# A graph-attention layer on one core: GpSimd multiplies the rows of the last three jobs by the first scale vector, with its drain behind that and one wait for each scattered tile

## The chip, the cores and the metric

The kernel runs on one core of a Trainium2 chip. The metric is the time of one execution in microseconds on the device. The kernel before was timed in three runs: 673.37, 671.60 and 670.68 us, median 671.6 us.

## The reference

Inputs are 10,000 nodes with rows of 512 floats and 5,000 edges (source, destination) sorted by destination. The layer is attention over the edges, followed by a residual block with layer norms (`n = 10000`, 8 heads of 64):

```python
q, k, v = [(h @ W).reshape(n, H, DK) for W in (Wq, Wk, Wv)]
e = jnp.einsum('ehd,ehd->eh', k[src], q[dst]) / np.sqrt(DK)
attn = softmax of e over the edges of one destination
a = jax.ops.segment_sum(attn[:, :, None] * v[src], dst, num_segments=n).reshape(n, DM)
o = a @ Wo
x = _layernorm(h + o, ln1_g, ln1_b)
f = jax.nn.relu(x @ W1 + b1) @ W2 + b2
y = _layernorm(x + f, ln2_g, ln2_b)
out = _layernorm(h + y)          # without scale and shift
```

(`attn` and the last two lines are written shorter here than in the program.) What matters below is the second half: a norm, a multiplication by `ln1_g`, a small two-layer network, a norm with `ln2_g` and `ln2_b`, the input row added, and a third norm.

## The kernel before

The work is cut into ten rounds of 500 edges. In a round TensorE turns the gathered rows of the destinations and sources, makes q, k, v and the output product O, and the vector and scalar engines do the softmax as scans along the edges. Then the rows go through the residual block in **jobs** of 250 rows, as two tiles of 125 partitions by 512 floats. A round has four jobs: E0 and E1 hold rows of edge destinations, which get the product O added; N0 and N1 hold rows of nodes without an edge. The rows of a job lie in the tile `rows` (`w[n]` in the code) and its input rows in `x_rows` (`xr[n]`), each one buffer for each of the four slots.

The steps of a job, with their lines: the input rows come by an indirect DMA from GpSimd (L575); `norm` or `norm9` makes the first norm (scalar engine L770, or vector engine L1062); `be` adds `ln2_b` to the input rows by an accumulating DMA from GpSimd (L657); `T` turns the normed rows (TensorE L1234) and the scalar engine copies them (L779); `xr` multiplies the rows by `g1_all`, the first scale vector, on the vector engine (L1068, 125x1024 floats at once); `F1` and `F2` are the network (L1263, L1271, and L1251 for the last three jobs) with a relu between them (L788); `x2` adds the network's result from PSUM to the rows (L1074); `sq` takes the squares (L735); `t` takes the mean off and multiplies by `g2_all` (L1083); `y` scales and adds `x_rows` (L1091); `sq3`, then `r3` (L1103), makes the last shift; `z` on the scalar engine (L800) or `z9` on the vector engine (L1097) makes the output rows, tile by tile; `out` scatters them by two indirect DMAs from GpSimd (L579). GpSimd also makes two tensor instructions a round for the softmax mask (L643, L645).

The order of the steps on each engine is written out by hand: the table `PLAN` gives each step ten numbers, one for each round, and an engine runs its steps sorted by them. A name that begins with ">" stands in the last round only, "<" in all but the last, "!" once. Each engine works strictly through its list; semaphores do the waiting between engines. The last three jobs of the program are E0, E1 and N0 of the last round, called **closing** in the code. Their network starts from PSUM banks that a matmul fills with the bias (`B9`, L1247).

`SETTLE` is one step of GpSimd, `pool.drain()` (L626). In the kernel before it stands behind the `be` steps of E0 and E1 of the last round and ahead of the `be` of N0.

The waits that matter below, before (arguments cut; for E1 and N0 of the last round, whose output rows the vector engine makes, the count is `last_rows_done`):

```python
elif what == "x2":
    on.wait_ge("xr_done", nth("dve.xr", slot, i))
elif what == "out":
    on.wait_ge("rows_done", nth("act.z", slot, i))
    for t in range(2):
        scatter(w_wide[n][:, t, :], ...)
```

Of the kernel before, what the change touches and what calls it, by code (L numbers as in the profile page):

```python
# [10 lines left out]
ALU = mybir.AluOpType  # L11
# [78 lines left out]
TXD2 1810 5453 11668 16099 22626 28648 34753 40873 48430 50827;  # L90
TXD3 2014 5783 11716 16147 22674 28987 34801 41303 48478 51070;
# [13 lines left out]
XP 5730 9620 16673 22431 28716 34700 40678 46625 53502 59318;  # L105
# [14 lines left out]
N1.sq 9890 16299 22722 28808 34869 40968 47486 53193 58293 62855;  # L120
<E0.norm 10033 15291 22025 28140 34146 40202 46290 52471 58617;
E1.sq1 10385 16847 22483 28505 34558 40731 47004 52864 59129 63242;
<E0.seed 10527 16746 22960 29055 35090 41733 47244 53401 58881;
N1.ln2 10628 16726 23061 29035 35024 41129 47641 53381 58455 63026;
<E0.T 10648 15710 22272 28358 34434 40562 46888 53006 58982;
E1.ln1 10744 17109 22864 28769 34849 40947 47166 53102 59298 63404;
N1.rs2 10764 17781 23429 29349 35483 41713 48269 53934 58862 63384;
E1.rs1 10836 17155 22915 29156 35070 41110 47199 53362 59513 63449;
<E1.norm 10901 17207 23100 29208 35200 41162 47345 53555 60009;
<E0.F1 11042 17129 22934 29369 35044 40921 47218 53336 59272;  # L130
# [4 lines left out]
N1.rs3 11592 19012 24685 30541 36907 43505 49604 54986 59796 64410;  # L135
# [5 lines left out]
N1.z 12265 19760 25120 31037 38553 43830 49841 55623 59867 64791;  # L141
<N0.seed 12407 18623 24895 30609 37617 43036 48955 55070 59533;
E1.sq 12507 18797 24704 30894 36927 43148 49104 54811 61590 64267;
E0.rs2 12699 18243 24996 30496 36135 42969 48409 55051 59848 64197;
<N0.F1 12770 18772 24611 30516 36427 42944 49315 55025 60463;
E0.sq3 12946 19306 25528 31581 37267 43363 49442 55343 60319 64429;
E0.ln3 13101 20418 25816 31796 37430 43573 49623 55534 60489 64592;
E0.rs3 13169 20451 26086 31829 37930 43762 50173 55603 60581 64933;
E0.z 13221 20576 26423 32292 38733 44282 50226 56199 60696 64985;
E1.ln2 13579 19032 25068 31776 37410 43343 49295 54966 61746 64572;  # L150
E1.rs2 13647 19149 25101 31945 37766 43971 49584 55171 61779 64612;
N0.sq 13857 20257 26105 31964 37998 44092 50516 56057 61159 64649;
E1.sq3 14148 20066 26280 32434 38289 44593 49983 55813 62035 65146;
N0.ln2 14290 20771 26260 32272 38533 44472 50875 56389 61450 64952;
E1.ln3 14310 20718 26565 32616 38444 44807 50934 56510 62190 65301;
N0.rs2 14331 20945 26585 32577 38694 44788 50914 56422 61571 65127;
N0.sq3 14508 21265 26808 32755 38875 45177 51266 56600 61798 65353;
N0.ln3 14671 21420 26964 32910 39037 45527 51550 56976 61953 65509;
E1.rs3 14691 20751 26604 32649 39018 45319 50967 56815 62223 65334;
N0.rs3 14730 21608 27126 32943 39070 45689 51712 57138 62243 65542;  # L160
<E1.z 15149 20803 26984 33010 39151 45547 51408 56996 62288;
# [22 lines left out]
TXD3 2224 5973 11788 16268 23238 29372 35247 41364 48549 51742;  # L184
# [135 lines left out]
def graph_attention(nc, x, src, dst, Wq, Wk, Wv, Wo, g1, be1, g2, be2, W1, b1, W2, b2, out):  # L320
# [7 lines left out]
    R = 125  # L328
# [979 lines left out]
```

## Time and profile before

| | |
|---|---|
| time, median of 3 runs | 671.6 us (670.68 to 673.37) |
| profiled execution, its own time | 670.29 us |
| its span, first to last instruction | 668.6 us |
| TensorE busy | 639.0 us (96%) |
| vector engine busy | 552.5 us (83%) |
| scalar engine busy | 497.8 us (74%) |
| GpSimd busy | 399.5 us (60%) |
| granted TensorE clock, mean | 0.988 of full |

The busy shares are of the span. Times in the text are microseconds from the first instruction of this execution. TensorE is busy nearly all the time until 650 us and not at all after that: the last 19 us are a tail of the three closing jobs and of N1, with the vector and scalar engines at work and GpSimd scattering. A GpSimd row in a timeline is the time in which it makes the descriptors of a DMA, not the transfer.

### The profile page before, as it was taken

To read this page: it belongs to the slowest core of one execution; us is meant where nothing else is said; L and a number is where in the kernel's file an instruction comes from. 1 tells how busy PE (TensorE), PEld (TensorE's weight loads), DVE (VectorE), ACT (ScalarE), POOL (GpSimd) and SP (SyncE) were. 2 spreads that over 40 slices of the span, in tenths; PEclk is the share of its full clock that TensorE was granted. 3 is DMA by queue.
4 is the path that set the end of the run, shared out by engine and by line. 5 is a ranking of instruction groups with operands and counts; after the bars stand their busy time and mean duration, and the time that the engine had idled before them with its cause. 6 is when DMAs were issued, how large, how long until landed. Compare 5 with 4: busy or idle time off the path is not lost.

```text
span 668.6 us, 10865 instructions
## 1 busy us (share of the span) xinstructions
PE 639.0 (96%) x3576; PEld 491.1 (73%) x3576; DVE 552.5 (83%) x1211; ACT 497.8 (74%) x1203; POOL 399.5 (60%) x363
## 2 busy tenths in 40 slices
PE   5999999999999999999999999999999999999980
PEld 3787877777787777777777777777787777777740
DVE  5848879878896898789979887997888799699884
ACT  3334347985868878888879689796987798699884
POOL 8567271665547665767678555566565853856515
PEclk9999999999999999999999999999999999999995
DMA  7864245553644592576464635454774643367553
GB/s 247 215 163 112 58 112 96 150 155 94 170 86 150 161 178 68 187 119 141 127 181 95 139 111 168 117 136 125 167 166 153 178 80 77 109 142 173 151 86 132
DMA packets 38801, 91.48 MB, mean 137 GB/s; under 512 B 9394, under 2 KB 10690, under 8 KB 38746
## 3 DMA queue, kind: packets, MB, share of 16 engines
q0 software_dynamic: 31536, 82.79, 49.5%
q1 hardware_dynamic: 7210, 8.01, 4.6%
q8 instruction: 28, 0.46, 0.3%
q14 instruction: 27, 0.22, 0.1%
HBM read 71.20 MB, written 20.99 MB: 138 GB/s over the span
## 4 chain that ended last, share of the span: by engine, by line
PE 85%; ACT 6%; DVE 3%; POOL 2%; issue 2%; DMA 1%; POOLq 0%; ACTq 0%; DVEq 0%
PE pP L1137 61%; PE pF L1271 5%; PE pT L1197 5%; PE pS L1263 5%; PE pT L1234 5%; ACT squares L735 2%; DMA x_rows<-in_x_dram,node_idx 1%; PE pS L1207 1%; ACT rows L800 1%; PE pS L1283 1%; POOL out_dram L579 1%; ACT nT L779 1%; PE pP L1283 1%; ACT rows L770 1%; POOL xd L575 1%
## 5 line engine op out<-in xcount | busy, mean ns | idle before, releaser
L735 ACT ACTIVATE squares<-rows,sums 125x512 bf16<-125x512 f32 x200 | 142.4, 715 | 28.9 <-DVE rows L1091 14.0
L575 POOL DMA_INDIRECT x_rows<-in_x_dram,node_idx x40 | 47.4, 1186 | 71.6 <-DVE rows L1091 51.3
L575 POOL DMA_INDIRECT x_rows<-in_x_dram,edge_idx x40 | 46.9, 1171 | 51.6 <-DVE rows L1091 28.3
L657 POOL DMA_DIRECT2D x_rows<-in_L_gnn_ln_b_dram x40 | 52.8, 1459 | 31.7 <-DVE rows L1003 12.2
L1137 PE MATMUL pP<-wo_hi,aT_hi 128*125 128x512 f32 x160 | 65.9, 412 | 0.0
L1137 PE MATMUL pP<-xTd_hi,wq_hi 128*128 128x500 f32 x160 | 64.3, 402 | 0.8 <-DVE xTd_lo L941 0.8
L1137 PE MATMUL pP<-xTs_hi,wv_hi 128*128 128x500 f32 x160 | 64.8, 405 | 0.0
L1137 PE MATMUL pP<-xTs_hi,wk_hi 128*128 128x500 f32 x160 | 63.1, 394 | 0.0
L1137 PE MATMUL pP<-wo_lo,aT_hi 128*125 128x512 f32 x160 | 63.1, 394 | 0.0
L1137 PE MATMUL pP<-xTs_hi,wk_lo 128*128 128x500 f32 x160 | 63.0, 393 | 0.0
L1137 PE MATMUL pP<-wo_hi,aT_lo 128*125 128x512 f32 x160 | 62.9, 393 | 0.0
L1137 PE MATMUL pP<-xTs_hi,wv_lo 128*128 128x500 f32 x160 | 62.6, 391 | 0.0
L1137 PE MATMUL pP<-xTd_hi,wq_lo 128*128 128x500 f32 x160 | 62.6, 391 | 0.0
L579 POOL DMA_INDIRECT out_dram<-rows,node_idx x40 | 45.8, 1145 | 27.8 <-ACT rows L800 16.6
L1137 PE MATMUL pP<-xTd_lo,wq_hi 128*128 128x500 f32 x160 | 62.3, 389 | 0.0
L1137 PE MATMUL pP<-xTs_lo,wk_hi 128*128 128x500 f32 x160 | 62.1, 388 | 0.0
L1137 PE MATMUL pP<-xTs_lo,wv_hi 128*128 128x500 f32 x160 | 62.1, 388 | 0.0
L1091 DVE SCALAR_TENSOR_TENSOR rows<-rows,rs,x_rows 125x512 f32<-125x512 f32 x80 | 57.2, 753 | 4.5 <-DMA x_rows<-in_L_gnn_ln_b_dram 1.8
L800 ACT ACTIVATE rows<-rows,shift,rs 125x512 f32<-125x512 f32 x76 | 57.4, 806 | 4.5 <-DVE shift L1103 4.4
L575 POOL DMA_INDIRECT xd<-in_x_dram,dst_idx x36 | 48.9, 1359 | 19.7 <-issue 10.2
L579 POOL DMA_INDIRECT out_dram<-rows,edge_idx x40 | 43.6, 1090 | 26.9 <-ACT rows L800 16.7
L1083 DVE SCALAR_TENSOR_TENSOR rows<-rows,nmean,g_all 125x512 f32<-125x512 f32 x80 | 56.6, 749 | 2.8 <-ACT squares L735 2.7
(190 smaller groups left out, 1721.0 us busy)
## 6 DMA issues: line engine op xcount, KB each, us to landing
x_rows<-in_L_gnn_ln_b_dram POOLq DMA_DIRECT2D x40, 512.0 KB, 7.2
dst_row<-in_dst_dram SPq DMA_DIRECT2D x9, 250.5 KB, 3.5
q<-in_L_gnn_Wq_dram SPq DMA_DIRECT2D x1, 1024.0 KB, 5.7
rows<-in_L_gnn_Wk_dram SPq DMA_DIRECT2D x1, 1024.0 KB, 9.0
rows<-in_L_gnn_Wv_dram SPq DMA_DIRECT2D x1, 1024.0 KB, 6.1
x_rows<-in_L_gnn_Wo_dram SPq DMA_DIRECT2D x8, 128.0 KB, 8.1
x_rows<-in_x_dram,node_idx POOLq DMA_INDIRECT x40, 3.6
edge_idx<-fill_nodes,fill_idx POOLq DMA_INDIRECT x40, 3.2
```

Of the source, the lines that this page charges most:

```text
L575: pool.indirect_dma_start(rows, None, x, bass.IndirectOffsetOnAxis(ap=table[:, column:column + 1].bitcast(U32), axis=0), bounds_check=N - ...
L579: pool.indirect_dma_start(out, bass.IndirectOffsetOnAxis(ap=table[:, column:column + 1].bitcast(U32), axis=0), rows, None, bounds_check=N ...
L657: pool.dma_start(xr_wide[n], bass.AP(tensor=be2.tensor, offset=be2.offset, ap=[[0, P], [0, 2], [1, D]]), accum_op=ALU.add).then_inc(s[f"be ...
L735: ins = act.activation(squares[:, t, :], w[n][:, t, :], ACT.Square, scale=-float(D), bias=sums[c][n][:, t:t + 1], accum_out=sq[c][n][:, t: ...
L800: ins = act.activation(w[n][:, t, :], w[n][:, t, :], ACT.Identity, scale=rs[3][n][:, t:t + 1], bias=shift[n][:, t:t + 1])
L1083: ins = dve.scalar_tensor_tensor(w[n][:, t, :], w[n][:, t, :], nmean[n][:, t:t + 1], g2_all[0:R, :], ALU.add, ALU.mult)
L1091: ins = dve.scalar_tensor_tensor(w[n][:, t, :], w[n][:, t, :], rs[2][n][:, t:t + 1], xr[n][:, t, :], ALU.mult, ALU.add, accum_out=sums[3][ ...
L1137: ins = pe.matmul(acc, left(a, k), right(b, k), start=(k == 0 and a == b), stop=(k == KC - 1 and a == 1))
L1197: ins = pe.transpose(pT_of(i, step)[:, R * t:R * t + R], rows[0:R, t, P * k:P * k + P], ident[0:R, 0:R])
L1234: ins = pe.transpose(pT_of(i, step, half)[:, 2 * R * c + R * t:2 * R * c + R * t + R], w[n][:, t, P * (2 * half + c):P * (2 * half + c) + ...
L1263: ins = pe.matmul(hidden(i, slot)[DFF * t:DFF * t + DFF, :], w1[:, k, :], nT[:, k, R * t:R * t + R], start=(k == 0), stop=(k == KC - 1))
L1271: pe.matmul(f_banks(i, slot)[t][0:R, :], hT_of(i, slot)[DFF * t:DFF * t + DFF, :], w2[DFF * t:DFF * t + DFF, :], start=False, stop=True, s ...
```

## The change

Three things are changed, and the numbers of some steps in `PLAN`, which leave the order on TensorE and the scalar engine as it was.

1. `xr` of E0, E1 and N0 in the last round goes from the vector engine to GpSimd, as a step `xr9` with the same operands (125x1024, both inputs in SBUF), counted on a new semaphore that `x2` of these jobs waits for.
2. On GpSimd the steps now stand E0.xr9, E1.xr9, N0.be, N0.xr9, SETTLE, where SETTLE, N0.be stood.
3. `z` and `z9` count each of their two tiles, and each scatter waits for its own tile. This holds for all ten rounds.

```diff
-E0.xr 10768 15670 22546 28841 34825 40884 47195 53117 59047 63190;
+<E0.xr 10768 15670 22546 28841 34825 40884 47195 53117 59047;
...
-E1.xr 11526 17991 23735 29917 36131 42296 48107 54331 60995 63745;
+<E1.xr 11526 17991 23714 29917 36131 42296 48107 54331 60995;
...
->SETTLE 63423
+>E0.xr9 63423;
+>E1.xr9 63722;
+>N0.xr9 64005;
+>SETTLE 64107
...
+    late_rows = [(i, step.split(".")[0]) for i, step in sequence("pool") if step.endswith(".xr9")]
...
     elif what == "z":
         for t in range(2):
-            ins = act.activation(w[n][:, t, :], ...)
-        ins.then_inc(s["rows_done"], 1)
+            act.activation(w[n][:, t, :], ...).then_inc(s["rows_done"], 1)
...
+    elif what == "xr9":
+        on.wait_ge("all_loaded", 32)
+        on.wait_ge("turned", 2 * nth("pe.T", slot, i))
+        pool.tensor_tensor(w[n], w[n], g1_all[0:R, :].rearrange("p (a d) -> p a d", a=1).broadcast_to([R, 2, D]), ALU.mult)\
+            .then_inc(s["last_xr_done"], 1)
     elif what == "out":
-        if ("dve.z", slot, i) in steps_done:
-            on.wait_ge("last_rows_done", nth("dve.z", slot, i))
-        else:
-            on.wait_ge("rows_done", nth("act.z", slot, i))
         for t in range(2):
+            if ("dve.z", slot, i) in steps_done:
+                on.wait_ge("last_rows_done", 2 * nth("dve.z", slot, i) + t - 1)
+            else:
+                on.wait_ge("rows_done", 2 * nth("act.z", slot, i) + t - 1)
             scatter(...)
...
     elif what == "x2":
-        on.wait_ge("xr_done", nth("dve.xr", slot, i))
+        if (i, slot) in late_rows:
+            on.wait_ge("last_xr_done", late_rows.index((i, slot)) + 1)
+        else:
+            on.wait_ge("xr_done", nth("dve.xr", slot, i))
```

How it moves the instructions on GpSimd, at the end of the program. The slots are N0, N1, E0, E1; a scatter of `rows,node_idx` is N1's or N0's, of `rows,edge_idx` E0's or E1's. The drain is no row in these lists. Before, it stands between the second and the third DMA of L657:

```order
L657 DMA x_rows<-in_L0_gnn_ln2_b_dram 128x2x512 [waits hx_done] x2
L657 DMA x_rows<-in_L0_gnn_ln2_b_dram 128x2x512 [waits n1_done]
L579 DMA out_0_dram<-rows,node_idx 10000x512 [waits rows_done]
L579 DMA out_0_dram<-rows,node_idx 10000x512
L579 DMA out_0_dram<-rows,edge_idx 10000x512 [waits rows_done]
L579 DMA out_0_dram<-rows,edge_idx 10000x512
L579 DMA out_0_dram<-rows,edge_idx 10000x512 [waits last_rows_done]
```

And with the change, where the drain stands behind the last multiplication (line numbers are four higher):

```order
L661 DMA x_rows<-in_L0_gnn_ln2_b_dram 128x2x512 [waits hx_done] x2
L666 TENSOR_TENSOR rows<-rows,g1_all 125x1024 [waits turned,all_loaded]
L666 TENSOR_TENSOR rows<-rows,g1_all 125x1024 [waits turned]
L661 DMA x_rows<-in_L0_gnn_ln2_b_dram 128x2x512 [waits n1_done]
L666 TENSOR_TENSOR rows<-rows,g1_all 125x1024 [waits turned]
L583 DMA out_0_dram<-rows,node_idx 10000x512 [waits rows_done] x2
L583 DMA out_0_dram<-rows,edge_idx 10000x512 [waits rows_done] x2
L583 DMA out_0_dram<-rows,edge_idx 10000x512 [waits last_rows_done] x2
```

The three multiplications stand where GpSimd had only the drain, N0's `be` comes after two of them, and every scatter row has its own wait.

On the vector engine, from `x2` of E0 (buffer 2) over `y` of N1 (1) and `t` of E0 to `x2` of E1 (3). Before:

```order
L1074 SCALAR_TENSOR_TENSOR rows,sums2_2<-pF1,rows 125x512 [waits f_filled,xr_done]
L1074 SCALAR_TENSOR_TENSOR rows,sums2_2<-pF0,rows 125x512 [waits f_filled]
L1068 TENSOR_TENSOR rows<-rows,g1_all 125x1024 [waits turned]
L1078 TENSOR_SCALAR nmean2<-sums2_2 125x2 [waits x2_done]
L1091 SCALAR_TENSOR_TENSOR rows,sums3_1<-rows,rs2_1,x_rows 125x512 [waits be_added_N1,rs2,t_done]
L1091 SCALAR_TENSOR_TENSOR rows,sums3_1<-rows,rs2_1,x_rows 125x512
L1083 SCALAR_TENSOR_TENSOR rows<-rows,nmean2,g2_all 125x512 [waits sq2,nm2]
L1083 SCALAR_TENSOR_TENSOR rows<-rows,nmean2,g2_all 125x512
L1074 SCALAR_TENSOR_TENSOR rows,sums2_3<-pP0,rows 125x512 [waits f_filled,xr_done]
L1074 SCALAR_TENSOR_TENSOR rows,sums2_3<-pP1,rows 125x512 [waits f_filled]
```

With the change:

```order
L1086 SCALAR_TENSOR_TENSOR rows,sums2_2<-pF1,rows 125x512 [waits f_filled,last_xr_done]
L1086 SCALAR_TENSOR_TENSOR rows,sums2_2<-pF0,rows 125x512 [waits f_filled]
L1090 TENSOR_SCALAR nmean2<-sums2_2 125x2 [waits x2_done]
L1103 SCALAR_TENSOR_TENSOR rows,sums3_1<-rows,rs2_1,x_rows 125x512 [waits be_added_N1,rs2,t_done]
L1103 SCALAR_TENSOR_TENSOR rows,sums3_1<-rows,rs2_1,x_rows 125x512
L1095 SCALAR_TENSOR_TENSOR rows<-rows,nmean2,g2_all 125x512 [waits sq2,nm2]
L1095 SCALAR_TENSOR_TENSOR rows<-rows,nmean2,g2_all 125x512
L1086 SCALAR_TENSOR_TENSOR rows,sums2_3<-pP0,rows 125x512 [waits f_filled,last_xr_done]
L1086 SCALAR_TENSOR_TENSOR rows,sums2_3<-pP1,rows 125x512 [waits f_filled]
```

One row, the multiplication of E1 (L1068), is gone, and `x2` waits for GpSimd's count in its place. The multiplication of E0 is gone in the same way ahead of this piece and that of N0 behind it; nothing else moves.

## Rows read from the trace of the kernel before

**Rows 1.** By stretch, the last: busy us of PE, PEld, DVE, ACT, POOL; clock, DMA share, GB/s

```profile
650.00:669.00 19.00, 0.00 (x0) 0.00 (x0) 9.40 (x25) 9.64 (x28) 8.44 (x8) 0.56 0.43 134
```

**Rows 2.** Section 4 of the page, the chain that ended last, by engine

```profile
PE 85%; ACT 6%; DVE 3%; POOL 2%; issue 2%; DMA 1%; POOLq 0%; ACTq 0%; DVEq 0%
```

**Rows 3.** Timeline of GpSimd (POOL), 632 to 669 us: start, length, instruction, idle before

```profile
633.88 2.76 POOL L657 DMA_DIRECT2D x_rows<-in_L_gnn_ln_b_dram  x2
647.84 1.20 POOL L657 DMA_DIRECT2D x_rows<-in_L_gnn_ln_b_dram  x1 [11.20 <-issue]
655.01 1.11 POOL L579 DMA_INDIRECT out_dram<-rows,node_idx  x1 [5.96 <-ACT rows L800]
656.41 1.43 POOL L579 DMA_INDIRECT out_dram<-rows,node_idx  x1 [0.30 <-issue]
...
663.31 0.98 POOL L579 DMA_INDIRECT out_dram<-rows,node_idx  x1 [0.30 <-issue]
664.60 0.98 POOL L579 DMA_INDIRECT out_dram<-rows,node_idx  x1 [0.30 <-issue]
```

**Rows 4.** Timeline of the vector engine (DVE), 632 to 669 us

```profile
638.68 1.00 DVE L1062 TENSOR_SCALAR rows<-rows,rs,nb 125x512 f32<-125x512 f32 x2
...
640.96 0.69 DVE L1074 SCALAR_TENSOR_TENSOR rows<-pF,rows 125x512 f32<-125x512 f32 x1 [1.27 <-PE pF L1251]
...
643.39 0.75 DVE L1091 SCALAR_TENSOR_TENSOR rows<-rows,rs,x_rows 125x512 f32<-125x512 f32 x1
...
644.73 1.41 DVE L1083 SCALAR_TENSOR_TENSOR rows<-rows,nmean,g_all 125x512 f32<-125x512 f32 x2
...
646.06 0.69 DVE L1074 SCALAR_TENSOR_TENSOR rows<-pP,rows 125x512 f32<-125x512 f32 x1
...
648.62 1.23 DVE L1068 TENSOR_TENSOR rows<-rows,g_all 125x1024 f32<-125x1024 f32 x1
...
649.88 0.69 DVE L1074 SCALAR_TENSOR_TENSOR rows<-pF,rows 125x512 f32<-125x512 f32 x1
...
660.27 1.00 DVE L1097 TENSOR_SCALAR rows<-rows,rs,shift 125x512 f32<-125x512 f32 x2
```

**Rows 5.** Timeline of the scalar engine (ACT), 632 to 669 us

```profile
647.40 0.72 ACT L735 ACTIVATE squares<-rows,sums 125x512 bf16<-125x512 f32 x1
...
651.23 0.72 ACT L735 ACTIVATE squares<-rows,sums 125x512 bf16<-125x512 f32 x1 [0.23 <-DVE rows L1074]
...
652.65 1.50 ACT L800 ACTIVATE rows<-rows,shift,rs 125x512 f32<-125x512 f32 x2
```

**Rows 6.** Timeline of TensorE (PE), 632 to 669 us

```profile
640.78 1.07 PE L1234 MATMUL pT<-ident,rows 125*128 125x125 f32 x8
...
648.57 1.13 PE L1251 MATMUL pF<-w,hT 64*125 64x512 f32 x4
```

**Rows 7.** The two drains on GpSimd's sequencer: ns min/median/max, start

```profile
L626 POOLq DRAIN  x1: 11954/11954/11954, 635.4 to 635.4; - x1
...
L336 POOLq DRAIN  x1: 799/799/799, 667.5 to 667.5; - x1
```

**Rows 8.** Tile x_rows, 630 to 669 us, landings; then the traffic of one microsecond

```profile
DMA to landing us min/median/max: 6.4/7.4/8.3
...
643.00:644.00 1.00, 1.00 (x18) 0.83 (x13) 1.00 (x3) 1.00 (x5) 0.00 (x0) 1.00 0.02 4
```

**Rows 9.** Timelines of POOL and DVE at 436 and at 202 us

```profile
436.17 0.63 POOL L643 TENSOR_SCALAR far<-nsame 128x500 f32<-128x500 f32 x1
436.25 1.09 DVE L1091 SCALAR_TENSOR_TENSOR rows<-rows,rs,x_rows 125x512 f32<-125x512 f32 x1
...
202.76 0.61 POOL L645 TENSOR_SCALAR nsame<-nsame 128x500 f32<-128x500 f32 x1
202.78 0.69 DVE L1074 SCALAR_TENSOR_TENSOR rows<-pF,rows 125x512 f32<-125x512 f32 x1 [1.59 <-PE pF L1271]
```

**Rows 10.** One line of GpSimd, a memset of one column

```profile
L595 POOL MEMSET eps_col<- x1: 99/99/99, 11.2 to 11.2; 128x1 f32 x1
```

More of the change, by code:

```diff
@@ new lines @@
+E0.ln3 13101 20418 25816 31796 37430 43573 49623 55534 60489 64586;
+E0.rs3 13169 20451 26086 31829 37930 43762 50173 55603 60581 64910;
+E0.z 13221 20576 26423 32292 38733 44282 50226 56199 60696 64962;
+E1.ln2 13579 19032 25068 31776 37410 43343 49295 54966 61746 64566;
+E1.rs2 13647 19149 25101 31945 37766 43971 49584 55171 61779 64606;
+N0.sq 13857 20257 26105 31964 37998 44092 50516 56057 61159 64626;
+E1.sq3 14148 20066 26280 32434 38289 44593 49983 55813 62035 65123;
+N0.ln2 14290 20771 26260 32272 38533 44472 50875 56389 61450 64929;
@@ L222 @@
 G2 6883 11707 19807 25839 32991 37180 44037 50514 57738 62263;
-N0.sum 6978 15086 22739 28241 33332 40308 46610 52459 57533 62648;
+N0.sum 6978 15086 22719 28241 33332 40308 46556 52431 57533 62648;
 N1.sum 7097 11847 19279 25139 31297 38205 43462 50087 54799 59980;
@@ new lines @@
+N1.r3 11713 19740 24783 30973 38331 43581 49636 55073 59828 64556;
+<N0.xr 12083 18222 23848 31417 36018 42541 49369 54445 60428;
+E1.x2 12303 18469 24418 30458 36533 42962 48679 54676 61225 64106;
+E0.t 12426 17794 24109 30782 35886 42830 48984 54919 59842 63925;
+E1.m2 12558 19025 24600 30653 36668 43454 49482 55332 61540 64364;
+E0.y 12791 18832 25382 30987 37046 43144 49235 55198 60118 64230;
+E0.r3 13201 20557 26232 31861 38355 44177 50206 55800 60613 64942;
+E1.t 13268 19458 25516 31869 37245 43664 49644 55351 61746 64564;
@@ L264 @@
+N0.x2 13552 19956 25648 31663 37830 43914 50273 55871 60797 64433;
+N0.m2 13734 20624 25851 31798 38363 44185 50578 56287 60979 64696;
+E1.y 13742 19606 26097 32138 38012 44043 49835 55542 61889 64707;
+N0.t 14012 20975 26260 32273 38430 44408 50795 56307 61407 64950;
+N0.y 14363 21119 26663 32609 38727 44960 51120 56454 61606 65136;
+E1.r3 14723 20783 26922 32983 39132 45280 51045 56847 62255 65343;
+N0.r3 15549 21708 27158 32975 39124 45796 51861 57671 62486 65551;
 >E0.norm9 62887;
 >E1.norm9 63501;
->E1.z9 65386;
@@ L267 @@
->N0.z9 65593
+>E1.z9 65363;
+>N0.z9 65570
 """,
@@ L799, in _ @@
                         for t in range(2):
[L800 to L802 removed]
+                            act.activation(w[n][:, t, :], w[n][:, t, :], ACT.Identity,
+                                                 scale=rs[3][n][:, t:t + 1], bias=shift[n][:, t:t + 1])\
+                                .then_inc(s["rows_done"], 1)
         @block.vector
```

175 lines of the change are left out of this document (75 added, 100 removed).

## The prediction

> **What bounds the kernel now.** Read the stretches first: until 650 us TensorE sets the pace, and in the last 19 us it has nothing to do, while the vector engine (DVE) is busy for 9.4 us, the scalar engine (ACT) for 9.6 and GpSimd for 8.4 [rows 1]. The chain of waits over the whole span is TensorE's to 85% [rows 2]. The change touches rounds 1 to 9 only by the finer wait of the scatters, and no row of TensorE waits for a scatter there, so I cost that part at nothing: what covers it is TensorE's own work. All that can move the time lies behind 635 us.
>
> There, read GpSimd from the end backwards. The eight last scatters start at 655.01, and each begins 0.30 us after the one before has ended, a pitch of 1.29 us; the last ends at 665.6 [rows 3]. They are a queue with no hole. The output rows of N0, which feed the seventh, are complete at 661.3 [rows 4], but that scatter starts at 663.31 [rows 3]: the data is 2 us early, the queue is the bound. So the end is the **start of the first scatter plus 10.6 us**. The first one waits for N1's `z`, two tiles on ACT from 652.65 to 654.15 [rows 5]. It starts 0.86 us later, the cost of the wait and of the issue.
>
> What sets 652.65 is ACT's list: squares of E1's `x2` from 647.40, of E0's `y`, then squares of N0's `x2` at 651.23, then `z` [rows 5]. Those wait for DVE, which does E0's `t` at 644.73, E1's `x2` at 646.06, E0's `y`, the multiplication of N0 at 648.62 and N0's `x2` at 649.88 [rows 4]. TensorE gives N0's product between 648.57 and 649.7 [rows 6], so `x2` of N0 can't come earlier whatever DVE is spared.
>
> **The scatter waits for its own tile.** `z` of N1 makes its first tile in half of 1.50 us. The first scatter can start 0.7 us earlier, if GpSimd is free and nothing else moves. The second tile is ready well before the second scatter. **Gain 0.7 us.**
>
> **The multiplications leave DVE.** Three times 1.15 us (1.23 busy at 648.62, less what overlaps with the next instruction [rows 4]). Before 640.96 DVE waited for TensorE 1.27 us anyway; of the second, 644.73 would become 643.97 at best, but E1's `x2` needs a product of TensorE that comes just before 646; the third is spared where TensorE holds `x2` back until 649.7 [rows 6]. **Gain at most 0.1 us**, and I count nothing.
>
> **The multiplications on GpSimd: length.** The trace has no tensor instruction with two inputs on GpSimd. The nearest is the mask, one input of 500 columns in 0.61 us [rows 9], with a fixed part of about 0.1 [rows 10]; so 0.5 us for 500 columns and 1.0 for 1024. With one read that is 1.1 us (lower end: 1.2 by plain proportion); if two inputs are read one behind the other 2.15; upper end 2.5, twice the plain proportion. I take **2.2 us**, because each column needs two reads. The Trainium skill (GPSIMD Engine Reference, Performance versus the Vector engine) gives 4497 ns for a two-input add of 2048 fp32 columns; half of it is 2.25 us, and the sum would then be 0.1 us larger.
>
> **What they block.** At 436.25 a DVE instruction with two inputs in SBUF took 1.09 us beside a mask of GpSimd that ended at 436.80, where the row at 643.39 takes 0.75: it began after the mask, and the next mask waited for it. At 202.78 `x2`, which reads PSUM and one SBUF operand, took its usual 0.69 beside the other [rows 4, 9]. So in this kernel `t`, `y`, `r1` and `r3` exclude a GpSimd tensor instruction, `x2` does not. The Trainium skill says this too (SBUF — State Buffer, SBUF: two separate sides): the port pair is an exclusive lock, "the other fully blocks". By a sharing of bandwidth the delays below would be small; by this rule they are whole instructions, and the trace agrees (1.09 against 0.75).
>
> Now walk through the tail, with 2.2 us for each:
> - E0: GpSimd is free at 636.64 [rows 3], multiplies until 638.85. E1's norm on DVE (638.68 to 639.68 [rows 4]) ends 0.4 later, at 640.1; TensorE turns those rows at 640.78 [rows 6]. Cost 0.
> - E1: its rows are turned at 641.85 [rows 6]; GpSimd works from 641.9 to 644.1. DVE's `y` of N1 starts at 644.2 in place of 643.39 [rows 4].
> - N0: `be` is issued first (1.25 us), to 645.4; then GpSimd waits for the second tile of `y` and works from 645.55 to 647.75. E0's `t` moves from 644.73 to 647.75: **3.0 us later**. E1's `x2` starts at 649.1 (+3.0), E0's `y` follows; N0's `x2` starts at 651.75, not 649.88 (+1.9, since the 1.15 us of its own multiplication is gone).
> - ACT: squares of E1 at 650.35 in place of 647.40, of E0's `y` at 651.9, then two logarithms and an exponential, and squares of N0 at 653.9, not 651.23. `z` of N1 starts at 655.3: **2.65 us later**. All behind it moves as much; N0's output tile is there at 663.5, the seventh scatter comes at 665.2.
>
> So the first scatter starts at 655.3 + 0.75 + 0.86 = 656.9, not 655.01: 2.65 - 0.7 = **1.9 us later**, and the queue of eight behind it is as long as before.
>
> **The drain.** Before, it stands for 11.95 us from 635.4, and GpSimd is held until 647.84 [rows 3, 7]. Nobody missed it. It now begins at 647.75, when N0's work is done, with the first scatter behind it. Two readings fit. (a) It waits for transfers: the last `be` was issued at 635.4 and landed within 8.3, at 643.7, where traffic ends [rows 8]; then 3.6 us pass to 647.34. With that, N0's `be`, issued near 644.1, lands at the latest at 651.5 (the median, 7.4 [rows 8]) and the drain ends by 655.1, the scatters could start at 655.6. It hides behind `z`. Cost 0. (b) Its 10.7 us after 636.64 are its own work. Then it ends at 658.45. The other drain, with ten DMAs since and all landed, took 0.8 us [rows 7], which fits either. I take (a), since the drain outlasts the transfers by so little; it isn't well founded.
>
> **Sum.** -0.7 - 0 + 2.65 + 0 = **+1.9 us**: the profiled execution of 670.3 us would be 672.2. It is 1.3 below the median of the runs, 671.6, so the forecast is **673.5 us**. A measurement here can tell about 0.5% (3.4 us) from no change; the forecast is slower, but within it.
>
> **Rivals.**
> 1. *The drain is work of its own (b), slower.* The first scatter starts at 658.45 + 0.5 = 658.95 (the 0.5 lies between the old drain's end and the next DMA), 2.0 after my forecast, but the queue then runs with less DVE work beside it: 7 pitches of 1.29 and 0.98 give 669.0 against 665.6, so +3.4 us, 675.0. With 2.5 us for a multiplication it is +4.0. For it: eleven us for some 350 DMAs and 0.8 for ten. Against it: why end just behind the landings? It decides as soon as the drain ends after 656.4. Chance 0.30.
> 2. *GpSimd and DVE don't hold each other up in this form, faster.* Then only the early tile is left: -0.7 us, 670.9. The 1.09 us row speaks against it. Chance 0.07.
> 3. *The multiplication is as fast as one read, 1.2 us.* E1's `x2` is then about 1 us late, N0's not at all; ACT's chain slips 0.6, the tile gives 0.7 back: 671.6, no change. Chance 0.08.
> 4. *It takes over 3 us*, E1's norm reaches TensorE late and both later ones grow: +4 to +5 us, 676. Chance 0.05.
> My forecast has the remaining 0.50.
>
> **The numbers.** The cases within 0.5% are the forecast (673.5, 2.5 us a piece gives 674.1), rivals 2 and 3, and nearly half of rival 1, which lies on the edge: 0.50 + 0.07 + 0.08 + 0.13, less 0.08 for a longer multiplication or a disturbed median, and less 0.03 for a gain I see no way to. That gives same 0.67, slower 0.30, faster 0.03. The range goes from rival 2, 670.8, to rival 1 at 2.5 us and some spread, 676.2.
>
> **What would show it.** In the profile after: three tensor instructions on GpSimd of about 2.2 us near 636.7, 641.9 and 645.6; E0's `t` starting when the third ends; a first scatter near 657 behind N1's first tile by 0.86. If the drain ends after that tile, rival 1 holds. If `t` of E0 starts at 644 and takes its usual 1.4 us, the exclusion is wrong. If the scatters have holes between them, the output rows and no longer the queue are the bound, and my sum is too small.

## The result and the profile after

The changed kernel takes 674.23 us (median of 22 runs), the kernel before 672.09 us in the runs beside it. The ratio is **1.0035, with a 95% interval of 1.002 to 1.0051**: by the ratio 2.4 us slower (the medians differ by 2.1), inside the 0.5% that the prediction called "same". The forecast was 673.5 us.

The profiled execution after has a span of 675.2 us, 6.6 more than the one of before. Not all of that is the change. This execution reached the turning of E0's rows in the last round at 638.24 us; other kernels below, which up to there are the same but for single steps off the chain, at 633.6 to 637.6. The start of the program shows most of the rest: long before the three jobs that are changed, TensorE was granted 0.94 of the full clock on average in one execution and all of it in the other, and in the same 60 us it got through 276 matmul instructions against 301. The first 60 us of the kernel after with the part of them at half the clock (1.2 and not 2.4 GHz), then the first 60 us of the kernel before, from the view by stretches (columns: start:end, length, busy us of PE, PEld, DVE, ACT, POOL with counts, granted TensorE clock, DMA share, GB/s):

```profile
0.00:60.00 60.00, 47.48 (x276) 38.21 (x277) 35.20 (x89) 18.53 (x33) 40.75 (x49) 0.94 0.75 191
...
42.79:49.62 6.83, 6.05 (x15) 4.87 (x16) 0.65 (x1) 0.72 (x2) 5.38 (x6) 0.50 0.64 166
```

```profile
0.00:60.00 60.00, 51.29 (x301) 41.32 (x302) 39.10 (x96) 21.52 (x39) 41.48 (x49) 1.00 0.69 191
```

The other executions fit this. Three, the one of before among them, have no such stretch of half clock near 43 us and reach the turning at 633.6 to 634.1; ten have one of 3.4 us and reach it at 635.5 to 637.6; this one has 6.8 us and reaches it at 638.24.

So I read everything from one mark: the start of TensorE's turning of E0's rows in the last round, 634.14 us before and 638.24 after:

```profile
634.14 1.02 PE L1234 MATMUL pT<-ident,rows 125*128 125x125 f32 x8
```

```profile
638.24 1.02 PE L1246 MATMUL pT<-ident,rows 125*128 125x125 f32 x8
```

Times "from the mark" below are differences to it, and **the stretch** is the time from it to the end of the last scatter: 31.44 us before, **34.07 after, +2.63**. It repeats to 0.01 us between executions of kernels that do the same there (34.07, 34.07, 34.07, 34.06 and 34.07 in five), where whole executions differ by 5 us. Behind the last scatter 2.9 to 3.0 us remain in both.

GpSimd after, from its timeline (columns as in [rows 3]):

```profile
639.50 1.24 POOL L661 DMA_DIRECT2D x_rows<-in_L_gnn_ln_b_dram  x1 [0.79 <-PE pT L1246]
640.29 2.84 POOL L666 TENSOR_TENSOR rows<-rows,g_all 125x1024 f32<-125x1024 f32 x1
646.08 2.38 POOL L666 TENSOR_TENSOR rows<-rows,g_all 125x1024 f32<-125x1024 f32 x1 [2.95 <-PE pT L1246]
648.39 1.19 POOL L661 DMA_DIRECT2D x_rows<-in_L_gnn_ln_b_dram  x1
649.17 2.80 POOL L666 TENSOR_TENSOR rows<-rows,g_all 125x1024 f32<-125x1024 f32 x1
661.67 1.12 POOL L583 DMA_INDIRECT out_dram<-rows,node_idx  x1 [9.70 <-ACT rows L809]
663.09 1.04 POOL L583 DMA_INDIRECT out_dram<-rows,node_idx  x1 [0.30 <-issue]
...
671.33 0.98 POOL L583 DMA_INDIRECT out_dram<-rows,node_idx  x1 [0.30 <-issue]
```

The row that has the engine to itself takes 2.38 us. The two of 2.84 and 2.80 us begin while the row of `be` ahead of them still runs; from its end they take 2.39 too. The eight scatters are a queue without a hole again.

The vector engine after (as [rows 4]; L1095 is `t`, L1090 `m2`, L1103 `y`, L1086 `x2`, L1071 the norm):

```profile
639.38 4.31 DVE L1095 SCALAR_TENSOR_TENSOR rows<-rows,nmean,g_all 125x512 f32<-125x512 f32 x2
...
643.86 1.00 DVE L1071 TENSOR_SCALAR rows<-rows,rs,nb 125x512 f32<-125x512 f32 x2
645.05 0.69 DVE L1086 SCALAR_TENSOR_TENSOR rows<-pF,rows 125x512 f32<-125x512 f32 x1 [0.19 <-PE pF L1263]
...
646.40 2.08 DVE L1090 TENSOR_SCALAR nmean<-sums 125x2 f32<-125x2 f32 x1
648.39 0.74 DVE L1103 SCALAR_TENSOR_TENSOR rows<-rows,rs,x_rows 125x512 f32<-125x512 f32 x1
...
649.06 3.47 DVE L1103 SCALAR_TENSOR_TENSOR rows<-rows,rs,x_rows 125x512 f32<-125x512 f32 x1
...
652.46 1.40 DVE L1095 SCALAR_TENSOR_TENSOR rows<-rows,nmean,g_all 125x512 f32<-125x512 f32 x2
653.79 0.68 DVE L1086 SCALAR_TENSOR_TENSOR rows<-pP,rows 125x512 f32<-125x512 f32 x1
...
656.36 0.16 DVE L1090 TENSOR_SCALAR nmean<-sums 125x2 f32<-125x2 f32 x1
656.43 0.68 DVE L1086 SCALAR_TENSOR_TENSOR rows<-pF,rows 125x512 f32<-125x512 f32 x1
```

Each multiplication on GpSimd has a long row beside it: `t` of N1 takes 4.31 us for two tiles (usual 1.41, [rows 4]), `m2` of E0, an instruction of two columns, 2.08 (0.16 at 656.36), and the **second tile of N1's `y` 3.47 (usual 0.75)**. Behind that come `t` of E0, `x2` of E1 at 15.55 us from the mark (11.91 before) and `x2` of N0 at 18.19 (15.74 before).

The scalar engine after (as [rows 5]; L744 are squares, L809 is `z`):

```profile
652.57 0.72 ACT L744 ACTIVATE squares<-rows,sums 125x512 bf16<-125x512 f32 x1 [3.09 <-DVE rows L1103]
...
655.12 0.72 ACT L744 ACTIVATE squares<-rows,sums 125x512 bf16<-125x512 f32 x1 [0.50 <-DVE rows L1086]
...
660.03 1.50 ACT L809 ACTIVATE rows<-rows,shift,rs 125x512 f32<-125x512 f32 x2
```

It waits 3.09 us for that second tile, then 0.50 for `x2` of E1, and from there it is busy without a gap until `z` of N1, which starts 21.79 us from the mark (18.51 before, +3.28). The first scatter starts 1.64 us after `z`, not 2.36, since it waits for one tile only. 3.28 less 0.72 is **+2.6 us**, the whole difference. No `x2` waited for GpSimd's product: E1's, at 653.79, is ready at 648.46, and N0's, at 656.43, at 651.97.

The two drains of GpSimd's sequencer after (as [rows 7]):

```profile
L630 POOLq DRAIN  x1: 9670/9670/9670, 648.8 to 648.8; - x1
```

```profile
L339 POOLq DRAIN  x1: 709/709/709, 674.3 to 674.3; - x1
```

The first ends at 658.52, 2.3 us before the first output tile is there. It costs nothing. Whether it waits for landings or has work of its own this row doesn't say: the landing of N0's `be`, 654.51, is 4.0 us before its end, and GpSimd was free 6.55 us before it.

### The profile page after: what moved, and what is told of

The parts are those of the page before. It is cut to its first block and busy times, and to the rows that moved or that the text cites. A ratio compares the mean times of both kernels' runs of the same rounds, so it can differ in the third digit from the quotient of the medians.

```text
span 675.2 us, 10866 instructions
## 1 busy us (share of the span) xinstructions
PE 639.8 (95%) x3576; PEld 491.9 (73%) x3576; DVE 555.9 (82%) x1208; ACT 497.6 (74%) x1203; POOL 409.6 (61%) x366
## 5 line engine op out<-in xcount | busy, mean ns | idle before, releaser
L744 ACT ACTIVATE squares<-rows,sums 125x512 bf16<-125x512 f32 x200 | 142.3, 715 | 31.2 <-DVE rows L1103 16.5
L1103 DVE SCALAR_TENSOR_TENSOR rows<-rows,rs,x_rows 125x512 f32<-125x512 f32 x80 | 59.7, 783 | 3.8 <-issue 1.4
L1095 DVE SCALAR_TENSOR_TENSOR rows<-rows,nmean,g_all 125x512 f32<-125x512 f32 x80 | 59.0, 778 | 2.8 <-ACT squares L744 2.6
L809 ACT ACTIVATE rows<-rows,shift,rs 125x512 f32<-125x512 f32 x76 | 57.4, 806 | 4.6 <-DVE shift L1115 4.4
L1086 DVE SCALAR_TENSOR_TENSOR rows<-pF,rows 125x512 f32<-125x512 f32 x78 | 50.4, 683 | 8.4 <-PE pF L1283 8.2
```

Of the source, the lines that this page charges most:

```text
L744: ins = act.activation(squares[:, t, :], w[n][:, t, :], ACT.Square, scale=-float(D), bias=sums[c][n][:, t:t + 1], accum_out=sq[c][n][:, t: ...
L809: act.activation(w[n][:, t, :], w[n][:, t, :], ACT.Identity, scale=rs[3][n][:, t:t + 1], bias=shift[n][:, t:t + 1])\
L1086: dve.scalar_tensor_tensor(w[n][:, t, :], f_banks(i, slot)[t][0:R, :], 1.0, w[n][:, t, :], ALU.mult, ALU.add, accum_out=sums[2][n][:, t:t ...
L1095: ins = dve.scalar_tensor_tensor(w[n][:, t, :], w[n][:, t, :], nmean[n][:, t:t + 1], g2_all[0:R, :], ALU.add, ALU.mult)
L1103: ins = dve.scalar_tensor_tensor(w[n][:, t, :], w[n][:, t, :], rs[2][n][:, t:t + 1], xr[n][:, t, :], ALU.mult, ALU.add, accum_out=sums[3][ ...
```

## The experiments

The theory was: a tensor instruction of GpSimd holds the vector engine up (exclusion), for its whole length, and the queue of eight scatters carries the delay of `z` to the end; the drain waits for landings and is hidden. The rivals: the delay comes from `x2` waiting for GpSimd's product; the drain is work of its own; nothing is excluded. The tile waits and the last kernel below were timed in twelve runs a series; the others ran once, and only their traces are read.

### The tile waits alone

The kernel before with the third part of the change: `z` and `z9` count each tile and each scatter waits for its own.

```diff
-ins.then_inc(s["rows_done"], 1)
+act.activation(w[n][:, t, :], ...).then_inc(s["rows_done"], 1)
...
+on.wait_ge("rows_done", 2 * nth("act.z", slot, i) + t - 1)
```

> The kernel before with the third part of the change alone: z and z9 count each tile, each scatter waits for its own tile, in all ten rounds. I read the stretch from TensorE's turning of E0's rows in the last round to the end of the last scatter, 31.44 us before and 34.07 after. My theory says the queue of eight scatters starts one tile of z earlier, so 30.7 us for the stretch and 20.2 us up to the first scatter (before 20.86), and the time 0.1% under the kernel before, 671.4 against 672.1. Rival: the first scatter is bound by something else near there, the stretch stays at 31.4. Second rival: the finer waits cost something in rounds 1 to 9, the time is 1 us or more longer.

Measured: the stretch 30.83 us, the first scatter at 20.16 from the mark (636.36 in this execution), the ratio to the kernel before 0.9989 (0.9967 to 1.0012).

```profile
656.51 1.11 POOL L579 DMA_INDIRECT out_dram<-rows,node_idx  x1 [5.94 <-ACT rows L800]
...
666.20 0.99 POOL L579 DMA_INDIRECT out_dram<-rows,node_idx  x1 [0.30 <-issue]
```

The gain in the stretch is 0.61 us, as foreseen to 0.1; in the time it can't be told from nothing. The other parts of the change therefore cost 34.07 - 30.83 = **3.24 us**, where the sum had 2.65.

### Multiplications on GpSimd that nobody uses

On top of the tile waits, the same three places on GpSimd hold a multiplication of the same form on an unused tile; the vector engine keeps its own three.

```diff
->SETTLE 63423
+>E0.dum9 63423;
+>E1.dum9 63722;
+>N0.dum9 64505;
+>SETTLE 64607
...
+elif what == "dum9":
+    on.wait_ge("turned", 2 * nth("pe.T", slot, i))
+    if slot != "E0":
+        on.wait_ge("dum_done", 1 if slot == "E1" else 2)
+    pool.tensor_tensor(q[0:R, 0:2, :], q[0:R, 2:4, :], g1_all..., ALU.mult).then_inc(s["dum_done"], 1)
```

> The kernel before with the tile waits, and on GpSimd, in the places of the change, three multiplications of the same form whose operands and result nobody else uses; the vector engine keeps its own three, and no x2 waits for GpSimd. The drain stands behind the third, and E0, E1 and N0 are worked out as before. If GpSimd's instruction holds the vector engine up by the port alone, t of N1, then the multiplication of E1 or y of N1, then y or t take 2 to 3 us longer than usual though nothing waits for a result: x2 of E1 comes 3.5 to 5 us later than in the kernel before (11.91 us after the turning of E0), and the stretch to the end of the last scatter is 34 to 36 us. If the delay of the change comes from x2 waiting for GpSimd's product, everything here runs as in the kernel before: x2 of E1 at 11.9, the stretch 30.7.

Measured: `x2` of E1 at 17.23 us from the mark, 5.3 later than before, the stretch 36.10, both a little above what I expected. In its timeline of the vector engine (L1090 `t`, L1085 `m2`, L1098 `y`):

```profile
638.51 3.91 DVE L1090 SCALAR_TENSOR_TENSOR rows<-rows,nmean,g_all 125x512 f32<-125x512 f32 x2
...
645.91 2.33 DVE L1085 TENSOR_SCALAR nmean<-sums 125x2 f32<-125x2 f32 x1
648.15 0.74 DVE L1098 SCALAR_TENSOR_TENSOR rows<-rows,rs,x_rows 125x512 f32<-125x512 f32 x1
...
648.83 3.46 DVE L1098 SCALAR_TENSOR_TENSOR rows<-rows,rs,x_rows 125x512 f32<-125x512 f32 x1
```

The same rows are long, with no data between the two engines. So it is the port, the engines' shared way to SBUF that the prediction speaks of, and not the product: `x2` waiting for GpSimd plays no part. It also shows that sparing the vector engine its three multiplications was worth something once GpSimd holds it up: with them the stretch is 2.0 us longer. Part of that is the other direction: the vector engine's multiplication of E1 had the port first, and GpSimd's second row took 3.40 us in place of 2.38.

### Writes on GpSimd that nobody uses

```diff
-pool.tensor_tensor(q[0:R, 0:2, :], q[0:R, 2:4, :], g1_all..., ALU.mult).then_inc(s["dum_done"], 1)
+pool.memset(q[:, :, :], 0.0).then_inc(s["dum_done"], 1)
```

> As the run with three dummy multiplications, but each dummy is a memset of 128x2048 of the same unused tile: GpSimd writes and reads nothing. Theory, if it is the reading of SBUF that excludes: instructions of the vector engine with two inputs in SBUF (t, y, the multiplications) keep their usual 0.67 to 0.75 us a tile, the stretch is 30.7 to 31.5. Rival: every GpSimd tensor instruction excludes them, then t of N1 and y of N1 are stretched by the length of the memset as in the profile after (4.31 us for two tiles of t, 3.47 for one of y), and the stretch is over 33.

Measured: the stretch 30.80. GpSimd and the vector engine in their timelines:

```profile
641.39 1.80 POOL L666 MEMSET q<- 128x2048 f32 x1 [3.46 <-PE pT L1240]
...
644.20 1.97 POOL L666 MEMSET q<- 128x2048 f32 x1
```

```profile
635.81 1.41 DVE L1090 SCALAR_TENSOR_TENSOR rows<-rows,nmean,g_all 125x512 f32<-125x512 f32 x2
...
642.79 0.43 DVE L1085 TENSOR_SCALAR nmean<-sums 125x2 f32<-125x2 f32 x1
642.86 0.75 DVE L1098 SCALAR_TENSOR_TENSOR rows<-rows,rs,x_rows 125x512 f32<-125x512 f32 x1
...
644.21 1.41 DVE L1090 SCALAR_TENSOR_TENSOR rows<-rows,nmean,g_all 125x512 f32<-125x512 f32 x2
```

`t` at 644.21 takes its 1.41 us beside a memset that runs from 644.20 to 646.17. An instruction of the vector engine with two inputs in SBUF is thus held up by a GpSimd instruction that reads SBUF, not by one that only writes it. The one with a single input, `m2`, ends at 643.22, 0.03 after the memset of 641.39 ends: it does seem to be held up by both. Beside GpSimd's instructions that read it is the same: with the changed kernel, the dummy multiplications and the one-input kernel below, `m2` ends 0.02 to 0.03 us behind GpSimd's instruction too. The Trainium skill (SBUF — State Buffer, SBUF: two separate sides) has both cases: two SBUF inputs collide "only against a GpSimd op that reads SBUF", a performance mode of the vector engine with any. The first the trace confirms with 1.41 against 4.31 us. For the second, against an instruction that only writes, this one row speaks, and that `m2` runs in such a mode isn't shown here.

### N0's multiplication behind N1's `y`

```diff
 on.wait_ge("turned", 2 * nth("pe.T", slot, i))
+if slot == "N0":
+    on.wait_ge("y_done", nth("dve.y", "N1", i))
 pool.tensor_tensor(w[n], w[n], g1_all..., ALU.mult)
```

> The changed kernel with N0's multiplication on GpSimd also waiting for both tiles of y of N1, the order that my prediction took for granted. y's second tile then takes its usual 0.75 us in place of 3.47, and t of E0 is behind the multiplication alone. GpSimd is free for it only at 11.34 us after the turning of E0's rows (be of N0), y ends at 11.5, so it ends at 13.9 and t starts then and not at 14.22: x2 of E1 at 15.2 (15.55 in the changed kernel), first scatter at 23.1, the stretch 33.75. Rival: t gets ahead of the multiplication, then x2 of E1 comes at 12.9 to 13.3 and N0's product is late instead, x2 of N0 at 16.3 or later, and the stretch is 32 to 33.

Measured: `x2` of E1 at 14.91, the first scatter at 22.80, the stretch 33.44. The vector engine (L1105 `y`, L1097 `t`, L1088 `x2`), then GpSimd:

```profile
646.64 0.74 DVE L1105 SCALAR_TENSOR_TENSOR rows<-rows,rs,x_rows 125x512 f32<-125x512 f32 x1
...
647.31 3.51 DVE L1097 SCALAR_TENSOR_TENSOR rows<-rows,nmean,g_all 125x512 f32<-125x512 f32 x2
650.74 0.68 DVE L1088 SCALAR_TENSOR_TENSOR rows<-pP,rows 125x512 f32<-125x512 f32 x1
```

```profile
647.54 2.72 POOL L668 TENSOR_TENSOR rows<-rows,g_all 125x1024 f32<-125x1024 f32 x1 [0.38 <-DVE rows L1105]
```

`y` is whole again (0.74), and while the semaphore travels to GpSimd one tile of `t` gets ahead as well. GpSimd ends 0.70 us later from the mark than in the changed kernel (14.43 against 13.73), but then only the second tile of `t` is left. The stretch is 0.63 us shorter, twice what I expected of it; I had left out the tile of `t`.

### One input instead of two

This kernel multiplies the rows of the last three jobs by the constant 1: the scale by `g1` is left out there.

```diff
-pool.tensor_tensor(w[n], w[n], g1_all[0:R, :].rearrange(...).broadcast_to([R, 2, D]), ALU.mult)
+pool.tensor_scalar(w[n], w[n], 1.0, 0.0, ALU.mult, ALU.add)
```

> The changed kernel with each of the three multiplications on GpSimd read from one tile instead of two: the rows times the constant 1, so the scale vector g1 is left out of the last three jobs. If the length of GpSimd's instruction is two reads of every column, it falls from 2.38 to 1.1 or 1.2 us, and with it what it blocks: x2 of E1 comes at 12.8 us after the turning of E0's rows (15.55 in the changed kernel, 11.91 before), x2 of N0 at 15.7 (18.19, 15.74), and the stretch is 31.0 to 31.5 us. If the length is the columns alone, it stays at 2.4 and the stretch at 34.07.

Measured: `x2` of E1 at 12.23, of N0 at 15.66, the stretch 30.79, a little under the range. GpSimd:

```profile
644.84 1.05 POOL L666 TENSOR_SCALAR rows<-rows 125x1024 f32<-125x1024 f32 x1 [4.21 <-PE pT L1246]
...
647.66 1.14 POOL L666 TENSOR_SCALAR rows<-rows 125x1024 f32<-125x1024 f32 x1 [0.62 <-PE pT L1246]
```

1.05 us for one input and 2.38 for two (the instruction is another kind as well, so the number of inputs isn't the only difference). At half the length nearly all of the cost is gone (0.04 us under the tile waits alone), because the delays fall into idle time of the vector engine; N0's `x2` waits for TensorE there, 0.71 us.

### Only E0's multiplication on GpSimd

```diff
 >E0.xr9 63423;
->E1.xr9 63722;
->N0.xr9 64005;
->SETTLE 64107
+>SETTLE 63424
```

E1 and N0 get their `xr` on the vector engine back. E1's `m2` stands ahead of N0's `xr` there, and not behind it as in the kernel before.

> The changed kernel with E0's multiplication alone on GpSimd, the drain right behind it and ahead of N0's be as in the kernel before, and E1 and N0 multiplied on the vector engine. E0's multiplication holds up t of N1 and the norm of E1 by about 2.9 us as in the changed kernel, but TensorE wanted E1's rows no earlier: x2 of E0 at 6.81 us and of E1 at 11.9 after the turning of E0's rows, the stretch 30.8 (30.83 with the tile waits alone). All of the loss would then belong to the other two. Rival: the delay of t and the norm costs something further on, x2 of E1 comes 0.5 to 1.5 us later and the stretch is 31.3 to 32.3.

Measured: the stretch 30.88, `x2` of E0 at 6.81 and of E1 at 11.92.

```profile
637.39 4.30 DVE L1093 SCALAR_TENSOR_TENSOR rows<-rows,nmean,g_all 125x512 f32<-125x512 f32 x2
...
641.88 1.00 DVE L1069 TENSOR_SCALAR rows<-rows,rs,nb 125x512 f32<-125x512 f32 x2
643.07 0.69 DVE L1084 SCALAR_TENSOR_TENSOR rows<-pF,rows 125x512 f32<-125x512 f32 x1 [0.19 <-PE pF L1261]
```

2.9 us of hold-up cost nothing up to `x2` of E1 (11.92 us from the mark, 11.91 with the tile waits alone). The 0.05 us of the stretch come behind it, where `m2` has the other place: `x2` of N0 is at 15.81 and not 15.73. Of the 2.9 us 1.14 us are the vector engine's own multiplication, which is gone, 1.08 come out of its wait for TensorE (1.27 us [rows 4], now 0.19), and the other 0.7 out of a wait for ACT ahead of the norm (0.67 in the run with dummy writes). The other two multiplications carry 3.19 of the 3.24 us, if not all.

### What the drain does

The next four kernels have the changed one's multiplications and differ from it in the drain. First without it:

```diff
 >N0.xr9 64005;
->SETTLE 64107
```

> The changed kernel without the drain behind the multiplications. If the drain waits for landings and costs nothing here, the stretch stays at 34.1 us (33.8 to 34.4), and the drain at the end of the program, which now has all DMAs of the kernel ahead of it, but all landed, still takes 0.7 to 0.8 us. If a drain is work of its own for the DMAs since the last one, the one at the end takes about 10 us and the stretch is shorter or the same.

The stretch is 34.07, but the span ends 9.36 us behind the last scatter and not 2.89. The last drain, with all DMAs landed at 673.4:

```profile
L338 POOLq DRAIN  x1: 7176/7176/7176, 673.6 to 673.6; - x1
```

Both readings of the prediction were incomplete: a drain can take long though everything has landed. The early drain takes 6.5 us off the end of the program. Then with the drain waiting until N0's `be` has landed:

```diff
 elif step == "SETTLE":
+    on.wait_ge("be_added_N0", 16 * ROUNDS)
     pool.drain()
```

> The changed kernel with its drain waiting for the landing of N0's be, so that every DMA ahead of it has landed when it starts. If it is own work of 6.55 us (about 340 DMAs since the start), it takes 6.5 to 7.2 us from the landing, 16.3 us after the turning of E0's rows, and ends at 22.9 to 23.5; the first scatter, 23.43 in the changed kernel, comes at 23.4 to 24.0 and the stretch is 34.1 to 34.7. If the drain only waits for landings and ends 3.6 to 4 us behind them, it takes 4 us or less, and the stretch stays at 34.07.

```profile
L631 POOLq DRAIN  x1: 6520/6520/6520, 649.7 to 649.7; - x1
```

6.52 us with nothing in flight. It ends 22.42 us from the mark and the stretch stays at 34.06: it is hidden even so, but by little. Then with a second drain in the middle of the program, and with that and the wait together:

```diff
+!SETTLE5 38000;
 >SETTLE 64107
```

> The changed kernel with a second drain of GpSimd in the middle of the program (near 38000 on the order's scale, about 400 us). So far the late drain ended 6.55 us after GpSimd was free in three kernels (changed, dummy reads, dummy writes) and 3.6 us after the last landing in two (before, tile waits), and without it the drain at the end of the program took 7.18 us with all DMAs landed. Theory: a drain is work in proportion to the DMAs since the last drain, some 20 ns each, in two parts, 2.95 us before it looks at the last landing and 3.6 behind it. Then the late drain, with about 40% of the DMAs before it, ends some 3 us after GpSimd is free or, if the landing (2.5 us after that) is what counts, 1.5 us behind the landing, and the one in the middle takes 4 us or, where it meets transfers in flight, longer. Rival: a fixed wait of a drain with DMAs in flight, then the late one ends 6.55 us after GpSimd is free as before. The stretch from the turning of E0's rows to the last scatter stays at 34.1 in both.

> The changed kernel with a second drain in the middle of the program, and the late one waiting for the landing of N0's be: 128 DMAs since the last drain, all landed. With 314 of them it took 6.52 us, with 322 at the end 7.18, with 8 0.70. If it is work in proportion to the DMAs, it takes 3.0 us (0.55 and 0.019 for each). If there is a fixed part for anything but a handful, it takes 3.6 or more, up to 6.5 where the number doesn't count. The stretch stays at 34.07 in all cases.

The late drain in the first ended 5.80 us after GpSimd was free. In the second it had 128 DMAs since the last one, all landed, and took 5.78 us; the one in the middle, behind 186, took 5.68:

```profile
L633 POOLq DRAIN  x2: 5682/5730/5778, 383.0 to 651.4; - x2
```

So it isn't in proportion to the DMAs, against my theory: 5.78 us for 128 of them, 6.52 for 314, 7.18 for 322, but 0.7 for 8. The 5.68 us aren't quite comparable: in the middle GpSimd was still at work on the mask for 0.6 us of them, and the last landing came 1.1 us after the start. All readings of the drain in the tail, us (DMAs counted in the order of the program):

```
kernel                DMAs since  GpSimd free  last landing
                      last drain   to its end   to its end
before                   313          10.70        3.61
tile waits               313          10.01        3.60
first tile ahead         313          10.02        3.61
the same again           313          10.20        3.60
E0 alone                 313           7.68        3.61
changed                  314           6.55        4.01
dummy reads              314           6.55        4.31
dummy writes             314           6.54        3.78
behind y                 314           6.55        4.91
one input                314           6.54        3.74
drain after landing      314            -          6.54
two drains, late         128           5.80        3.64
two drains, landed       128            -          5.80
```

("First tile ahead" is the kernel of the next section.) Two numbers fit all with 313 or 314: the drain ends **6.55 us after GpSimd is free for it or 3.6 us after the last landing, whichever is later**. In "drain after landing" GpSimd is free for it only when its wait is over, and the 6.5 us count from there. What they consist of, and why 8 DMAs cost so little and 128 so much, stays open.

### One more tile of `z` brought forward

The stretch is a queue behind `z` of N1, so I moved the first tile of `z` ahead of the squares of N0's `x2` on the scalar engine, and N1's `r3` ahead of N0's `x2` on the vector engine, on top of the tile waits. All multiplications are the vector engine's.

```diff
 elif what == "sq":
+    if slot == "N0" and i == ROUNDS - 1:
+        on.wait_ge("shifted", nth("dve.r3", "N1", i))
+        act.activation(w[1][:, 0, :], w[1][:, 0, :], ACT.Identity, ...).then_inc(s["rows_done"], 1)
     on.wait_ge("x2_done", 2 * nth("dve.x2", slot, i))
...
 elif what == "z":
     on.wait_ge("shifted", nth("dve.r3", slot, i))
     for t in range(2):
+        if slot == "N1" and i == ROUNDS - 1 and t == 0:
+            continue
...
-N1.r3 11713 19740 24783 30973 38331 43581 49636 55073 59828 64637;
+N1.r3 11713 19740 24783 30973 38331 43581 49636 55073 59828 64500;
```

> The kernel before with the tile waits, and with the first tile of N1's z ahead of the squares of N0's x2 on the scalar engine (and N1's r3 ahead of N0's x2 on the vector engine). The first scatter then starts about 1.6 us earlier than with the tile waits alone, 18.5 us after the turning of E0's rows, the second 1.1 us behind the second tile of z, and the later ones are bound by the output rows of E1 and N0, which come 0.5 us later than before: the stretch is 30.3 us (tile waits alone 30.83, before 31.44). If the output rows of N0 slip by a whole z, 30.9 or more, and nothing is won. The time differs from the kernel before by 0.2%, which the runs may not tell.

> The kernel with the tile waits and N1's first tile ahead once more, for its time: its stretch is 1.42 us shorter than the kernel before's, 0.21% of the time. If that is all that differs, the ratio lies at 0.998 and both series together may tell it from 1; if the finer waits cost something in the other rounds, at 0.999 to 1.000. The stretch is 30.0 again.

Measured: the first scatter at 18.41 and the stretch 30.02 us in both, 1.42 under before and 4.05 under the changed kernel. The ratio to the kernel before is 0.9988 (0.9968 to 1.0008) in the first series and 0.9981 (0.9964 to 0.9999) in the second. The queue now has holes:

```profile
654.79 1.11 POOL L579 DMA_INDIRECT out_dram<-rows,node_idx  x1 [4.18 <-ACT rows L748]
656.88 1.05 POOL L579 DMA_INDIRECT out_dram<-rows,node_idx  x1 [0.98 <-ACT rows L806]
...
661.56 0.98 POOL L579 DMA_INDIRECT out_dram<-rows,edge_idx  x1 [0.58 <-DVE rows L1102]
```

It waits for the second tile of N1 and for E1's output, so the queue and the output rows bound it about equally. This version beats the changed kernel clearly and the kernel before by some 0.15%, which one of the two intervals separates from nothing.

## Why the prediction was right, and where it was off

- **What bounds the kernel**: right. The eight scatters are a queue without a hole in both, with the same 10.6 us; the first scatter's start set the end (+2.57 at the first, +2.63 at the last).
- **The scatter waits for its own tile, -0.7**: 0.61 by itself.
- **The multiplications leave DVE, 0**: with GpSimd doing nothing in their place this wasn't tried. Where GpSimd holds the port they are worth 2.0 us (36.10 against 34.07).
- **Length 2.2 us**: 2.38, and the working (two reads for each column) fits: 1.05 with one input. The 2.25 us worked out from the Trainium skill (GPSIMD Engine Reference, Performance versus the Vector engine) was nearer, and low by 0.13 too.
- **What they block**: right in kind, shown by the dummies. It named `t`, `y`, `r1` and `r3`; `t` and `y` were held up, `r1` and `r3` never stood beside a multiplication of GpSimd, and `m2`, with one input in SBUF, is held up as well. For the first multiplication I had the norm of E1 end 0.4 us later; `t` of N1 ahead of it was held up by 2.9 us and the norm ended 1.08 later. Its cost of 0 stands all the same (`x2` of E1 at 11.92).
- **The step that was wrong**: "then GpSimd waits for the second tile of `y`". The order at the port was the other way: GpSimd's third instruction had it first and the second tile of `y` waited 2.7 us. So `t` of E0 came 3.6 us later and not 3.0, `x2` of N0 2.45 and not 1.9, `z` of N1 3.28 and not 2.65. That is nearly all of the gap between the +1.9 of the sum and the +2.6 of the stretch: GpSimd's third product was done at 13.73 us from the mark, where the walk had 13.61, and `t` could start only at 14.22, behind the rest of `y`. With the wait that makes the order so, the first scatter starts 1.94 us later than before. That the agreement is so close is partly luck, since there GpSimd ended later than I had it and a tile of `t` ran ahead.
- **The drain, cost 0**: right in the cost, wrong in both readings. (a) took the landing as the only cause; with everything landed it still takes 6.5 us. (b) took 10.7 us as its own work, where 6.5 are needed with everything landed. The prediction counted some 350 DMAs and ten, where the table has 313 and the end of the program 9; and the 651.5 that it called the latest landing of N0's `be` goes by the median of 7.4 us, not by the 8.3 (measured: 6.1 us from its start). Rival 1 fell, but not by far: a drain had to end some 22.9 us from the mark to hold the first scatter up (23.43 less the 0.5 behind a drain), and it ended at 20.3, or at 22.4 where it waited for the landing. What the early drain saves at the end of the program, 6.5 us, I had not seen at all; it didn't matter because the change keeps it.
- **Rivals 2 to 4**: no exclusion fell with the dummies, and over 3 us for a multiplication with the 2.38. The short multiplication was put at no change; made so short by its one input, it leaves the stretch 0.65 us under the kernel before, which is what the tile waits give.
- **The time**: +2.6 us in the stretch on 672.1 is 674.7; the runs show +2.4 in the ratio and 674.23. The forecast of 673.5 was low by 0.7 us. It started from a median of 671.6, 0.5 under the 672.09 of the runs beside the changed kernel, and its +1.9 was too small by 0.2 to 0.7 (2.1 between the medians, 2.4 in the ratio, 2.6 in the stretch).

## To carry to other kernels

Work given to GpSimd isn't free because GpSimd is idle: an instruction there that reads SBUF holds up the vector engine's instructions with two inputs in SBUF (and here the small `m2`) for its whole length, so 2.4 us there in place of 1.15 us on the vector engine is a loss wherever the vector engine is next on the path, and free only in a stretch where both then wait for a third. To cost such a step, list which instruction stands at the port when it starts, and take the worse order. And if a small change moves a tail, measure the tail from a mark in the trace: it repeats to 0.01 us where whole executions scatter by 5.

## What I had not expected of the hardware

- **A GpSimd instruction can hold the port before its own row starts.** The second tile of `t` of N1 began about 640.05 (639.38 and one tile of 0.67) in the changed kernel, the row of the multiplication at 640.29, in the middle of the row of `be` that ends at 640.74. Still `t` had to wait until 643.13, the multiplication's end: 0.67 + 3.08 + 0.56 are the 4.31 us. The second tile of `y` lost in the same way, 649.06 against 649.17. In both cases the multiplication stood behind `be`. It isn't `be` itself that holds the port: in the kernel before a tile of `y` ran beside the `be` that starts at 647.84 [rows 3] and took its usual time.

```profile
647.95 0.75 DVE L1091 SCALAR_TENSOR_TENSOR rows<-rows,rs,x_rows 125x512 f32<-125x512 f32 x1
```

And where the multiplication came long behind `be` ("behind N1's `y`"), a tile of `t` that began at 647.31, 0.23 us ahead of GpSimd's row, kept the port. Why the row starts late isn't shown.

- **A drain costs 0.7 to 0.8 us after 8 or 9 DMAs and 5.8 to 7.2 us after 128 or more, with all of them landed**, and behind 128 or more it ended no earlier than 3.6 us after the last landing. It is cheap only where the engine has time, and a drain at the end of the program is paid in full: 9.36 us behind the last scatter without the early one, 2.89 with it.
